# A chunk chain started behind its last input, row scalings moved from VectorE to ScalarE, and chunk states written and read back in parts

## The chip, the core and the metric

The kernel runs on one core of one Trainium2 chip. The engines named below are TensorE (PE in the profile), VectorE (DVE), ScalarE (ACT), GpSimd (POOL) and SyncE (SP), which here only issues DMAs. The metric is the device time of one execution in microseconds (us), as the median of several runs; lower is better.

## What is computed

One layer, all in float32: `x = x + attention(layernorm(x))`, then `x = x + ffn(layernorm(x))`, for 4 sequences of 1024 tokens and 128 features. The attention is a gated delta rule with 16 heads of 8 features, a recurrence over the tokens on an 8x8 state for each head:

```
def step(S, inp):
    qt, kt, vt, at, gft = inp
    bs1 = einsum('bhk,bhkv->bhv', kt, S)
    S1 = S + at[..., :, None] * bs1[..., None, :]
    S2 = exp(gft)[..., None] * S1
    bs2 = einsum('bhk,bhkv->bhv', kt, S2)
    S3 = S2 + at[..., :, None] * bs2[..., None, :] + kt[..., :, None] * vt[..., None, :]
    return (S3, einsum('bhk,bhkv->bhv', qt, S3))
_, o = lax.scan(step, S0, ...)
z = zeros_like(o)
out = stack([z, z, o], axis=2).reshape(B, 3 * N, H, HD)[:, -N:]
out = layernorm(out * gate) * ln_w @ Wout
...
# ffn: 16 experts, one for each token, and a shared one
scores = sigmoid(logits) * one_hot(top_1(logits))
masked_inputs = scores.T[:, :, None] * x[None, :, :]
gate, up = split(masked_inputs @ gate_up_proj[e])
expert_out = (up * silu(gate)) @ down_proj[e]
shared = silu(x @ w_gate.T) * (x @ w_up.T) @ w_down.T
```

Because of the stack and the slice, only the last 342 tokens' `o` are used, and they land in every third output row. In the other two thirds of the rows ("others") the attention adds nothing, so their FFN can run before the attention has ended. The rows that get an `o` are called "mixed".

## The kernel before, in words

**Chunks.** Each sequence is cut into 32 chunks (`C`), so that 4 x 32 chunks fill the 128 partitions. A chunk has 21 tokens of the first part (`L1`) and 11 of the second (`L2`), 32 steps (`NT`) in all. What a chunk does to the state that enters it is an 8x8 matrix and an added sum for each head, and these don't depend on the entering state. So 32 steps build all chunks' matrices and sums at once, in region 0 (21 steps) and in region 1 (11 steps). The last step ends with VectorE writing the last matrices (`next_state`, L1451, tile `state`), GpSimd multiplying the last sums (L978) and TensorE adding them up (`add_sum`, L1839); ScalarE then copies the sums out (`copy_sums`, L845), and SP stores and reloads matrices and sums through DRAM (L612 to L629).

**The chunk chain.** 63 serial steps m = 1 to 63 then carry the true state from chunk to chunk. For each, VectorE multiplies (L1527, from `ch_m` and `ch_s` to `ch_pr`) and reduces (L1532, to the next column of `ch_s`); GpSimd copies the chunk's sum into `ch_pr` (L1088). The copy for step m may go once step m-2 is reduced, since `ch_pr` has two buffers. Steps 1 to 32 use region 0's matrices (loaded some 80 us earlier), steps 33 to 63 region 1's. At the end the 32 states at which the second part begins, columns 0 to 31 of `ch_s`, go to DRAM and back in another layout into `state` (L1094, L1099, both issued by GpSimd), and the 11 steps with outputs begin (`products`, L1405; on TensorE `forward`, L1931 to L1934).

**What runs beside it.** The 22 tiles of "others" rows (128 rows of 128) are handled in six groups, five of 4 tiles and one of 2, by the shared expert: TensorE transposes the rows (L1798), ScalarE copies them (L830), TensorE multiplies by gate and up weights in two halves (L1810, L1811), ScalarE takes the silu (L835), VectorE multiplies (`shared_h`, L1296), TensorE multiplies by the down weights (L1820) and VectorE adds to the result (`shared_add`, L1301). VectorE's part is put between chain steps by `beside(m - 3)`: in every five steps of the chain, from m = 3 on, two `shared_h` and, two steps later, one `shared_add`. From m = 36 on, every third step has a `gate` (L1310 twice) of the expert pairs `RUNS[0]`, 12 pairs, of which the last two come after step 63.

**The rows that go to the experts.** Each of the 22 tiles is scaled by its score (L1500, VectorE, ahead of the chain) into room in `decayed` (8 tiles, part of the tile `grown`), `vterm` (8, part of `uv`) and `state` (6), and scattered by an indirect DMA that GpSimd issues (`scatter_tile`, L993), one behind each of GpSimd's first 22 chain copies. SP loads the expert pairs (L509) when all 22 scatters have landed; TensorE starts them (L1868) when the last `shared_add` is done.

**What sets the order.** Every engine runs its own program in the order in which it is written, and waits for semaphores. There is no scheduler. Ahead of the chain, ScalarE waits for `s_bout`, the landing of the stored sums (L625), and TensorE for `s_bc`, the copy of the sums. VectorE waits for `s_ba`, the last `add_sum`, because `vterm` is read by it.

## Time and profile before

| | us |
|---|---|
| median of 3 runs | 670.8 |
| lowest, highest | 670.62, 671.29 |
| the profiled execution's own time | 673.13 |
| its span, first to last instruction | 671.4 |
| chunk chain with what stands ahead of it, last state written to first product | 320.48 to 431.24 |

The span is what the profile's rows add up to. A row of the timeline gives the start, the duration (with merged instructions as one piece), the engine, the line, and in brackets how long the engine had been idle and which instruction ended that. The chain of waits is followed back from the last instruction, each step to what released it.

### The profile page before, as it was taken

The numbers are of one execution on the slowest core, as the hardware profiler recorded it, in microseconds if no ns is written. First come the engines' busy times: TensorE is split into PE (matmuls) and PEld (weight loads), VectorE is DVE, ScalarE is ACT, GpSimd is POOL, SyncE is SP. The second block draws the span as 40 slices with busy tenths as digits, with TensorE's granted clock in tenths as the row PEclk, the third lists the DMA queues.
The fourth block names the chain that finished last, engine by engine and source line by source line (L and its number), as shares of the span: only waits on it lengthen the run. The fifth ranks groups of instructions, "written<-read, shape, count | busy, mean of one in ns | idle before, by whom it ended". The sixth has DMA issues, their size and how long they took to land.

```text
span 671.4 us, 7382 instructions
## 1 busy us (share of the span) xinstructions
PE 528.3 (79%) x1809; PEld 273.7 (41%) x1810; DVE 492.5 (73%) x809; ACT 248.9 (37%) x515; POOL 360.0 (54%) x349
## 2 busy tenths in 40 slices
PE   1768989999999886877387689879999967578930
PEld 1434434444454433322154455525454255345520
DVE  3369999989898998799589999498999775412201
ACT  1825754444445242111122145533545124135520
POOL 4235767666667575654567333366767574700023
PEclk9868999999999998887799799998999977979985
DMA  9601116700000590000611012300100021112224
GB/s 218 138 0 32 32 42 162 217 0 1 0 1 0 141 356 35 1 0 0 170 35 55 17 48 69 110 15 16 31 23 18 0 52 35 43 56 63 63 80 111
DMA packets 46706, 41.79 MB, mean 62 GB/s; under 512 B 4588, under 2 KB 40248, under 8 KB 46168
## 3 DMA queue, kind: packets, MB, share of 16 engines
q1 hardware_dynamic: 43140, 35.61, 18.9%
q0 software_dynamic: 2400, 5.38, 2.7%
q10 hardware_dynamic: 1136, 0.46, 0.3%
q8 instruction: 12, 0.20, 0.1%
q14 instruction: 18, 0.15, 0.1%
HBM read 23.80 MB, written 17.63 MB: 62 GB/s over the span
## 4 chain that ended last, share of the span: by engine, by line
DVE 33%; PE 30%; issue 16%; POOL 12%; DMA 5%; ACT 2%; ACTq 1%; POOLq 0%; DVEq 0%; SPq 0%
DVE grown L1412 9%; PE ps L1874 6%; DVE early L1527 5%; POOL grown L1062 4%; DVE ps L1451 4%; PE ps L1831 4%; PE ps L1891 3%; DVE early L1532 3%; PE ps L1832 2%; PE ps L1931 2%; DVE grown L1439 2%; POOL uv L978 2%; PE ps L1639 2%; DVE grown L1405 2%; POOL early L1009 2%
## 5 line engine op out<-in xcount | busy, mean ns | idle before, releaser
L1062 POOL TENSOR_TENSOR grown<-grown 128x512 f32<-128x512 f32 x64 | 80.8, 1272 | 101.4 <-DVE grown L1439 101.4
L1412 DVE TENSOR_TENSOR grown<-ps,steps 128x1536 f32<-128x1536 f32 x64 | 112.1, 1752 | 1.8
L1831 PE MATMUL ps<-grown,cst 128*128 128x512 f32 x128 | 77.7, 692 | 27.8 <-DVE grown L1412 27.6
L857 ACT ACTIVATE uv<-ps 128x512 f32<-128x512 f32 x64 | 38.1, 597 | 110.5 <-DVE grown L1439 110.5
L1874 PE MATMUL ps<-steps 128*128 x128 | 69.6, 642 | 8.8 <-issue 8.6
L1832 PE MATMUL ps<-grown,cst 128*128 128x512 f32 x128 | 71.4, 641 | 0.0
L978 POOL TENSOR_TENSOR uv<-uv,steps 128x512 f32<-128x512 f32 x64 | 67.7, 1081 | 1.7 <-ACT uv L857 1.6
L1310 DVE TENSOR_TENSOR e_h<-rk,ps 128x256 f32<-128x256 f32 x64 | 25.4, 417 | 53.8 <-ACT rk L870 34.0
L1839 PE MATMUL ps<-uv,cst 128*128 128x512 f32 x128 | 60.4, 594 | 0.4 <-POOL uv L978 0.4
L1117 POOL TENSOR_TENSOR early<-state,qT 128x512 f32 x22 | 37.2, 1690 | 32.4 <-DVE state L1426 32.4
L1088 POOL COPY early<-early 128x32 f32<-128x32 f32 x63 | 27.5, 436 | 43.9 <-DVE early L1532 43.9
L1439 DVE TENSOR_TENSOR grown<-ps,steps 128x512 f32<-128x512 f32 x64 | 43.3, 677 | 9.3 <-PE ps L1831 9.2
L1831 PEld LDWEIGHTS ps<-grown,cst 128*128 128x128 f32 x128 | 22.7, 208 | 62.4 <-DVE grown L1412 56.2
L1451 DVE TENSOR_TENSOR ps<-ps,grown 128x512 f32<-128x512 f32 x60 | 41.6, 694 | 8.4 <-POOL grown L1062 8.4
L1445 DVE TENSOR_TENSOR ps<-ps,steps 128x512 f32<-128x512 f32 x64 | 44.1, 690 | 2.7 <-PE ps L1832 2.7
L1009 POOL DMA_INDIRECT early<-ys_mixed,slots_mixed x11 | 10.5, 959 | 64.8 <-DMA ys_mixed<-e_y 61.8
L1832 PEld LDWEIGHTS ps<-grown,cst 128*128 128x128 f32 x128 | 26.8, 209 | 35.4 <-issue 35.4
L1527 DVE TENSOR_TENSOR early<-early 128x256 f32<-128x256 f32 x63 | 39.4, 626 | 1.3
L870 ACT ACTIVATE rk<-ps 128x256 f32<-128x256 f32 x64 | 23.9, 384 | 40.7 <-PE ps L1874 39.7
L1891 PE MATMUL ps<-steps,e_hT 128*128 x256 | 35.9, 283 | 2.7 <-ACT e_hT L874 2.7
L1839 PEld LDWEIGHTS ps<-uv,cst 128*128 128x128 f32 x128 | 24.2, 190 | 31.8 <-issue 29.8
L1891 PEld LDWEIGHTS ps<-steps,e_hT 128*128 128x128 f32 x256 | 31.5, 191 | 9.1 <-issue 8.0
(221 smaller groups left out, 1001.8 us busy)
## 6 DMA issues: line engine op xcount, KB each, us to landing
steps<-gate_up_proj SPq DMA_DIRECT2D x1, 4096.0 KB, 15.3
xs_others<-zeros SPq DMA_DIRECT2D x1, 2496.0 KB, 10.9
steps<-xs_others SPq DMA_DIRECT2D x19, 128.0 KB, 2.1
ys_others<-e_y SPq DMA_DIRECT2D x19, 128.0 KB, 1.9
early<-chain_m SPq DMA_DIRECT2D x4, 512.0 KB, 6.3
xf<-x SPq DMA_DIRECT2D x4, 495.0 KB
normed<-early SPq DMA_DIRECT2D x28, 64.0 KB, 1.7
xs_mixed<-zeros SPq DMA_DIRECT2D x1, 1728.0 KB, 8.9
```

Of the source, the lines that this page charges most:

```text
L978: return G.tensor_tensor(wide(dst, w), wide(src, w), per_col(tile, k, 1, h, w), ALU.mult)
L1062: G.tensor_tensor(decayed[:, h], decayed[:, h], work[:, h, 1], ALU.add).then_inc(s_add[h], 1)
L1412: V.tensor_tensor(grown[:, :, h].rearrange("p e (x w) -> p e x w", w=HD), st, per_col(tile, FF, 3, h, HD), ALU.mult).then_inc(s_prod[h], 1)
L1439: V.tensor_tensor(wide(work[:, h, 1], HD), wide(ps[h][:, 1], HD), per_col(tile_of(i), PP, 1, h, HD), ALU.mult).then_inc(s_uterm[h], 1)
L1445: V.tensor_tensor(wide(bank[2 * h], HD), wide(bank[2 * h], HD), per_col(tile_of(i), K, 1, h, HD), ALU.mult).then_inc(s_term[h], 1)
L1451: V.tensor_tensor(dst, bank[2 * h], decayed[:, h], ALU.add).then_inc(s_state[h], 1)
L1527: V.tensor_tensor(ch_pr[:, m % 2, :, :, 0:HD], ch_m[r][:, :, i, :].rearrange("p j i -> p i j").unsqueeze(1) .to_broadcast([P, 4, HD, HD]), ...
L1831: T.matmul(bank[2 * h + 1], c["block"], work[:, h, 1], start=True, stop=True).then_inc(s_usum[h], 1)
L1832: T.matmul(bank[2 * h], c["minus"], work[:, h, 0], start=True, stop=True).then_inc(s_red[h], 1)
L1839: T.matmul(bank[4 + h], c["ident"], vterm[:, h], start=i in (0, L1), stop=i + 1 in (L1, NT)).then_inc(s_ba[h], 1)
L1874: T.matmul(b_gu(run, b)[u], e_xT[:, b, u], gu[:, bass.ds(ex * (2 * F), 2 * F)], start=True, stop=True).then_inc(s_eg, 1)
L1891: ins = T.matmul(b_y(run)[:, u * D:(u + 1) * D], e_hT[:, u, f * P:(f + 1) * P], dw[:, bass.ds(ex[u] * F + f * D, D)], start=(f == 0), stop ...
```

## The change

1. The 22 scalings leave VectorE. ScalarE does them (`scaled_rows`): four behind the first group's copy of the transposed rows, and four (at last two) behind the two silus of each group.
2. VectorE's wait for `s_ba`, `s_score` and `s_rows` ahead of the chain is gone; it waits for the last states and the loaded x, and begins the chain.
3. ScalarE no longer waits for `s_bout`. It waits instead for both last states, the scores and the rows. A silu on one column (`warm`) stands ahead of `copy_sums`.
4. TensorE's wait for `s_bc` moves behind the shared expert; its first gate matmul waits for the last states and the last copies of region 1.
5. GpSimd's scatters stand behind the copies of steps 2 to 5, 6 to 9, 11 to 14, 16 to 19, 21 to 24, 26 and 27 (`SCATTER_AT`), rather than behind 1 to 22.
6. The chunk states go out in three parts: columns 0 to 15 behind copy 50, 16 to 27 behind copy 62, 28 to 31 at the end. They come back in two: 0 to 15 behind copy 54, 16 to 31 at the end. VectorE waits for both (32 rather than 16).

```diff
@@ scalar engine
+            def scaled_rows(lo):
+                q = fb[OTHERS.name]
+                for j in range(lo, min(lo + 4, OTHERS.n)):
+                    if j == 4 * HALF // D:
+                        act.wait_ge(s_mout, 32)
+                    S.activation(q["scaled"][j], q["shared"][j], ACT.Copy, scale=q["score"][:, j:j + 1]).then_inc(s_sc, 1)
+
             def shared(t):
...
                         S.activation(xT_shared(t, g), b_xT(t, g)[:, 0:w], ACT.Copy).then_inc(s_fx, 1)
+                        if g == 0:
+                            scaled_rows(0)
                     for k in (0, 1):
...
                         S.activation(f_silu[t.name][:, 0:w], b_gate[k][:, 0:w], ACT.Silu).then_inc(s_fsg, 1)
+                    if t is OTHERS:
+                        scaled_rows(4 * g + 4)
...
                 front(i)
+            S.activation(warm[:, 2:3], eps[:], ACT.Silu)
             copy_sums(ucopy)
-            act.wait_ge(s_bout, 32)
+            for h in (0, 1):
+                act.wait_ge(s_state[h], NT + 2)
+            act.wait_ge(s_score, 1)
+            act.wait_ge(s_rows, 16 * 6 * B)
@@ gpsimd
+            SCATTER_AT = [j + 2 if j < 4 else SHARED_EVERY * (j // 4) + j % 4 + 1 for j in range(OTHERS.n)]
+            ENDS = (0, C // 2, C - 4, C)
+
+            def starts_out(k):
+                cols = slice(4 * ENDS[k], 4 * ENDS[k + 1])
+                G.dma_start(scr["s"].rearrange("(l i) x -> l i x", i=HD)[:, :, cols],
+                            ch_s[:, :, ENDS[k]:ENDS[k + 1], :].rearrange("l i c v -> l i (c v)")).then_inc(s_sout, 16)
+
+            def starts_in(lo, hi):
+                cols = slice(4 * ENDS[lo], 4 * ENDS[hi])
+                pool.wait_ge(s_sout, 16 * hi)
+                pool.wait_ge(s_mout, 32)
+                pool.wait_ge(s_scat[OTHERS.name], 16 * OTHERS.n)
+                G.dma_start(state[:].rearrange("p v (b x) -> p (v b) x", b=B)[:, :, cols],
+                            scr["s"].rearrange("(g q) x -> q g x", q=P)[:, :, cols]).then_inc(s_chout, 16)
...
-                if m <= OTHERS.n:
-                    scatter_tile(OTHERS, m - 1)
+                if m in SCATTER_AT:
+                    scatter_tile(OTHERS, SCATTER_AT.index(m))
+                if m == C + ENDS[1] + 2:
+                    starts_out(0)
+                if m == C + ENDS[1] + 6:
+                    starts_in(0, 1)
+                if m == C + ENDS[2] + 2:
+                    starts_out(1)
             pool.wait_ge(s_ca, 2 * C + 1)
-            pool.wait_ge(s_mout, 32)
-            G.dma_start(scr["s"].rearrange("(l i) x -> l i x", i=HD),
-                        ch_s[:, :, 0:C, :].rearrange("l i c v -> l i (c v)")).then_inc(s_sout, 16)
-            pool.wait_ge(s_sout, 16)
-            pool.wait_ge(s_scat[OTHERS.name], 16 * OTHERS.n)
-            G.dma_start(state[:].rearrange("p v (b x) -> p (v b) x", b=B),
-                        scr["s"].rearrange("(g q) x -> q g x", q=P)).then_inc(s_chout, 16)
+            starts_out(2)
+            starts_in(1, 3)
@@ vector engine
-            dve.wait_ge(s_score, 1)
-            dve.wait_ge(s_rows, 16 * 6 * B)
             dve.wait_ge(s_xf, 16 * 3 * B)
             for h in (0, 1):
-                dve.wait_ge(s_ba[h], NT + 1)
                 dve.wait_ge(s_state[h], NT + 2)
-            q = fb[OTHERS.name]
-            for j in range(OTHERS.n):
-                if j == 4 * HALF // D:
-                    dve.wait_ge(s_mout, 32)
-                V.tensor_scalar(q["scaled"][j], q["shared"][j], q["score"][:, j:j + 1], None, ALU.mult
-                                ).then_inc(s_sc, 1)
...
-            dve.wait_ge(s_chout, 16)
+            dve.wait_ge(s_chout, 32)
@@ tensor engine, shared(t)
                 if t is OTHERS:
                     transposes(0)
+                    for h in (0, 1):
+                        pe.wait_ge(s_state[h], NT + 2)
+                        pe.wait_ge(s_uc[h], NT + 1)
...
+            shared(OTHERS)
             pe.wait_ge(s_bc, 2)
-            shared(OTHERS)
```

On ScalarE, from the last copy of the last step to the second group. Before:

```order
L857 ACTIVATE uv<-ps 128x512 [waits s_bp0,s_uterm0]
L845 ACTIVATE uv<-ps 128x1024 [waits s_ba1,s_bp1,s_bp0,s_ba0]
L830 ACTIVATE grown<-ps 128x512 [waits s_b_out,s_f_transposed]
L835 ACT_TABLE_LOAD
L835 ACTIVATE grown<-ps 128x512 [waits s_f_gate_up]
L835 ACTIVATE grown<-ps 128x512 [waits s_f_h,s_f_gate_up]
L830 ACTIVATE grown<-ps 128x512 [waits s_f_transposed]
```

And in the changed kernel, where L858 is the copy of the sums, L839 that of the transposed rows, L831 the scaling and L846 the silu:

```order
L870 ACTIVATE uv<-ps 128x512 [waits s_bp0,s_uterm0]
L872 ACT_TABLE_LOAD
L872 ACTIVATE warm<-eps 128x1
L858 ACTIVATE uv<-ps 128x1024 [waits s_ba1,s_bp1,s_bp0,s_ba0]
L839 ACTIVATE grown<-ps 128x512 [waits s_rows_in,s_score,s_state0,s_state1,s_f_transposed]
L831 ACTIVATE grown<-early,score_others 128x128 x4
L846 ACTIVATE grown<-ps 128x512 [waits s_f_gate_up]
L846 ACTIVATE grown<-ps 128x512 [waits s_f_h,s_f_gate_up]
L831 ACTIVATE grown<-early,score_others 128x128 x4
L839 ACTIVATE grown<-ps 128x512 [waits s_f_transposed]
```

The table load moved ahead of the sums' copy, the wait for the stored sums (`s_b_out`) is gone, and eight scalings stand in the first group's stretch.

On VectorE, from the last state to the first `shared_h`. Before:

```order
L1451 TENSOR_TENSOR state<-ps,grown 128x512 [waits s_add0,s_term0,s_m_out]
L1500 TENSOR_SCALAR grown<-early,score_others 128x128 [waits s_state0,s_ba0,s_ba1,s_xf,s_state1,s_rows_in,s_score]
L1500 TENSOR_SCALAR grown<-early,score_others 128x128 x7
L1500 TENSOR_SCALAR uv<-early,score_others 128x128 x8
L1500 TENSOR_SCALAR state<-early,score_others 128x128 [waits s_m_out]
L1500 TENSOR_SCALAR state<-early,score_others 128x128 x5
L1515 MEMSET early 128x8x4
L1527 TENSOR_TENSOR early<-early 128x32x8 [waits s_sums_in,s_matrices_in,s_chain_state,s_uc1,s_uc0]
L1532 TENSOR_REDUCE early<-early 128x4x8 [waits s_chain_sums,s_chain_mul]
```

In the changed kernel (L1486 is the state, L1551 and L1556 the chain's multiplication and reduction, L1331 `shared_h`):

```order
L1486 TENSOR_TENSOR state<-ps,grown 128x512 [waits s_add0,s_term0,s_m_out]
L1539 MEMSET early 128x8x4 [waits s_state1,s_state0,s_xf]
L1551 TENSOR_TENSOR early<-early 128x32x8 [waits s_sums_in,s_matrices_in,s_chain_state,s_uc1,s_uc0]
L1556 TENSOR_REDUCE early<-early 128x4x8 [waits s_chain_sums,s_chain_mul]
L1551 TENSOR_TENSOR early<-early 128x32x8 [waits s_chain_state]
L1556 TENSOR_REDUCE early<-early 128x4x8 [waits s_chain_sums,s_chain_mul]
L1551 TENSOR_TENSOR early<-early 128x32x8 [waits s_chain_state]
L1556 TENSOR_REDUCE early<-early 128x4x8 [waits s_chain_sums,s_chain_mul]
L1331 TENSOR_TENSOR grown<-grown,ps 128x512 [waits s_f_silu]
```

The 22 scalings are gone; the chain's steps and the first `shared_h` behind step 3 stand as before.

On GpSimd, at the end of the chain. Before:

```order
L993 DMA xs_others<-state,slots_others 4992x128 [waits s_scaled]
L1088 COPY early<-early 128x32 [waits s_chain_state,s_sums_in] x41
L1094 DMA chain_s<-early 1024x1x128 [waits s_m_out,s_chain_state]
L1099 DMA state<-chain_s 128x8x128 [waits s_scattered_others,s_s_out]
L1106 UNCONDITIONAL_BRANCH [waits s_scattered_others]
```

In the changed kernel (L1010 the scatter, L1123 the copy, L1103 a part out, L1112 a part in):

```order
L1010 DMA xs_others<-state,slots_others 4992x128 [waits s_scaled]
L1123 COPY early<-early 128x32 [waits s_chain_state,s_sums_in] x23
L1103 DMA chain_s<-early 1024x1x64
L1123 COPY early<-early 128x32 [waits s_chain_state,s_sums_in] x4
L1112 DMA state<-chain_s 128x8x64 [waits s_scattered_others,s_m_out,s_s_out]
L1123 COPY early<-early 128x32 [waits s_chain_state,s_sums_in] x8
L1103 DMA chain_s<-early 1024x1x48
L1123 COPY early<-early 128x32 [waits s_chain_state,s_sums_in]
L1103 DMA chain_s<-early 1024x1x16 [waits s_chain_state]
L1112 DMA state<-chain_s 128x8x64 [waits s_scattered_others,s_m_out,s_s_out]
```

Three of the five transfers stand among the chain's copies; the one that is left to go out at the end has rows of 16 elements (64 bytes) rather than 128, and the one that comes back rows of 64.

## Rows read from the trace of the kernel before

**Rows 1.** The page's first row.

```profile
span 671.4 us, 7382 instructions
```

**Rows 2.** Chain of waits from the last state on: start, duration, what.

```profile
319.79 0.70 DVE state L1451
...
324.63 8.07 DMA chain_b<-uv
332.81 0.61 ACT grown L830
```

**Rows 3.** Timeline of that stretch: start, duration, instruction, [idle before <-releaser].

```profile
320.82 2.16 PE L1839 MATMUL ps<-uv,cst 128*128 128x512 f32 x4 [0.42 <-POOL uv L978]
321.74 0.24 POOL L1088 COPY early<-early 128x32 f32<-128x32 f32 x1
323.01 1.02 ACT L845 ACTIVATE uv<-ps 128x1024 f32<-128x1024 f32 x1 [4.08 <-PE ps L1839]
323.27 1.78 DVE L1500 TENSOR_SCALAR grown<-early,score_others 128x128 f32<-128x128 f32 x8 [2.79 <-PE ps L1839]
323.85 1.19 POOL L993 DMA_INDIRECT xs_others<-grown,slots_others  x1 [1.87 <-DVE grown L1500]
...
337.90 0.69 DVE L1296 TENSOR_TENSOR grown<-grown,ps 128x512 f32<-128x512 f32 x1 [6.61 <-ACT grown L835]
...
340.27 0.69 DVE L1296 TENSOR_TENSOR grown<-grown,ps 128x512 f32<-128x512 f32 x1 [0.64 <-ACT grown L835]
```

**Rows 4.** Stretches: length, busy of PE, PEld, DVE, ACT, POOL; PEclk, DMA share, GB/s.

```profile
325.00:327.00 2.00, 0.00 (x0) 0.00 (x0) 2.00 (x12) 0.00 (x0) 1.29 (x3) 1.00 0.99 229
333.00:335.00 2.00, 1.54 (x2) 0.84 (x3) 0.00 (x0) 1.69 (x2) 0.64 (x1) 0.50 0.51 133
422.70:425.20 2.50, 2.50 (x17) 1.82 (x15) 0.84 (x2) 1.64 (x4) 0.00 (x0) 1.00 0.85 256
```

**Rows 5.** Timeline of the shared expert's second group and the start of its third.

```profile
342.90 1.02 PE L1810 MATMUL ps<-grown,wT 128*128 128x512 f32 x2
344.82 0.60 ACT L835 ACTIVATE grown<-ps 128x512 f32<-128x512 f32 x1 [4.09 <-PE ps L1811]
346.67 0.60 ACT L835 ACTIVATE grown<-ps 128x512 f32<-128x512 f32 x1 [1.25 <-DVE grown L1296]
350.12 1.02 PE L1810 MATMUL ps<-grown,wT 128*128 128x512 f32 x2
```

**Rows 6.** ScalarE's scalings of the mixed rows, late in the kernel: timeline.

```profile
559.23 3.32 ACT L964 ACTIVATE early<-early,score_mixed 128x128 f32<-128x128 f32 x11
```

**Rows 7.** Groups by line, 338.5 to 421.4: busy us, mean ns | idle before, releaser.

```profile
L1527 DVE TENSOR_TENSOR early<-early 128x256 f32<-128x256 f32 x60 | 37.5, 626 | 1.1
L1532 DVE TENSOR_REDUCE early<-early 128x32 f32<-128x288 f32 x60 | 27.3, 454 | 2.1
```

**Rows 8.** Timeline: first pair's load and transposes, and the chain's end.

```profile
367.03 0.90 SPq L509 DMA_DIRECT2D steps<-xs_others  x2
379.98 0.66 PE L1868 MATMUL ps<-cst,steps 128*128 128x128 f32 x2 [1.39 <-DVE xf L1301]
...
420.94 0.45 DVE L1532 TENSOR_REDUCE early<-early 128x32 f32<-128x288 f32 x1
421.69 0.92 POOL L1094 DMA_DIRECT2D chain_s<-early  x1 [1.80 <-DVE early L1532]
431.24 3.27 DVE L1405 TENSOR_TENSOR grown<-state,steps 128x1024 f32<-128x1024 f32 x2 [2.18 <-DVEq L1540]
432.61 1.10 PE L1931 MATMUL ps<-grown,cst 128*128 128x512 f32 x2 [0.76 <-DVE grown L1405]
```

**Rows 9.** DMA issues: out<-in, queue, count, KB each, us from issue to landing.

```profile
chain_s<-early POOLq DMA_DIRECT2D x1, 512.0 KB, 4.1
state<-chain_s POOLq DMA_DIRECT2D x1, 512.0 KB, 4.9
...
xs_others<-state,slots_others POOLq DMA_INDIRECT x6, 2.3
```

More of the change, by code:

```diff
@@ L205, in build @@
         eps = sb("eps", [P, 1])
+        warm = sb("warm", [P, 3])
         early = sb("early", [P, L2 * COLS])
```

## The prediction

> **What bounds the kernel now.** I read the chain of waits first, since it names the stretch that the change touches. It runs from the last state (written at 319.79, done at 320.48) not into the chunk chain but into a store: the sums land 8.07 us after their issue at 324.63, and only then does ScalarE copy the first transposed rows, at 332.81 [rows 2]. The timeline shows what that does to VectorE [rows 3]. It idles 2.79 us from its last state until TensorE's last `add_sum` has ended (320.82 + 2.16 = 322.98), scales 22 tiles, and makes three chain steps. Then it stands 6.61 us in front of the first `shared_h`, which starts at 337.90, and 0.64 us in front of the second at 340.27. Behind that VectorE is full: in 60 steps its chain instructions take 37.5 + 27.3 us with 1.1 and 2.1 us of idle time before them [rows 7]. So from 340.27 to the last reduction's end at 421.39 [rows 8] VectorE sets the pace, and all that is won ahead of the first `shared_h` should arrive at the end of the chain. The stretch behind it is two DMAs in series: issue at 421.69, 4.1 us, issue again, 4.9 us, first product at 431.24 [rows 8, 9]. The last expert pairs run beside them on TensorE: it is free at 432.61 - 0.76 = 431.85 [rows 8].
>
> **Part 1, the start of the chain (edits 1 to 4): 10.65 us.** The first `shared_h` needs the later of two paths.
>
> The silu's path. ScalarE copies the sums from 323.01 to 324.03 as now, since that waits for TensorE until 322.98 and not for anything that changed. The 1.3 us table load and the one-column silu sit in the 4.08 us that ScalarE is idle before it [rows 3]. The transposes of the first rows have nothing but 322.98 ahead of them and four small matmuls to do, so they are done before 324.03. The copy of the rows takes 0.61 [rows 2]: 324.64. From TensorE's first gate matmul to the silu's start are 1.92 us in the second group (344.82 - 342.90), and the silu takes 0.60 [rows 5]. So: 324.64 + 0.03 + 1.92 + 0.60 + 0.05 = 327.25. The four scalings lie in ScalarE's wait for those matmuls: 11 took 3.32 us, 0.30 each, so four end at 324.64 + 1.25 = 325.9, before the silu could start at 326.6 [rows 6].
>
> GpSimd's path. Its copy for step 3 now stands behind the first scatter, and this waits for the first scaling, ready at 325.0. The first scatter took 1.19 and a copy 0.24 [rows 3], and a reduction 0.45 [rows 7]. So: 325.0 + 1.2 + 0.25 + 0.1 + 0.45 = 327.0. Steps 1 and 2 are done by then: step 1 can't be reduced before its copy, which GpSimd does at 321.74 as now [rows 3], and two steps of 1.16 us follow.
>
> The later path gives 327.25 against 337.90: **10.65 us** earlier. It matters that TensorE is at full clock. In the trace the granted clock is still 1.00 (2.4 GHz) at 325 to 327, with TensorE idle, and 0.50 (1.2 GHz) at 333 to 335, where the first gate matmuls ran [rows 4]. The changed kernel has them at 324.7 to 328.1, so I take the full clock; the other case is a rival.
>
> **Part 2, the second `shared_h`: 0.6 us.** Its wait of 0.64 came from those slow matmuls. At full clock the second silu starts at 324.67 + 2 x 1.72 + 0.2 = 328.3 and ends at 328.9. VectorE comes there 2.37 - 0.64 = 1.73 us after the first one's start, at 328.98 [rows 3]. So the wait goes: 0.6.
>
> **Part 3, the steady groups: 0.** What is added to ScalarE in each group is 1.25 us between the second silu and the copy for the next group. That silu ends at 347.27, so the copy would end at 347.27 + 1.25 + 0.61 = 349.1; TensorE is busy with the down weights until 350.12 anyway [rows 5]. That cover is 1.0 us; without it each of five groups would be late by the rest. GpSimd's scatters fall from five in five steps to four. The last one moves from copy 22 to copy 27, five steps and three products or some 8 us later; SP, whose next work is the pairs' load, has it at 367.03 now and would have it at about 375, while TensorE needs it at 379.98 [rows 8]: 2 us of cover with the load itself. The 22 scalings leave VectorE, but that is in part 1 and is not counted twice.
>
> **Part 4, the parts that go out and back among the chain's steps: 0.** Three more issues of 0.92 each on GpSimd [rows 8]. Behind copies 50, 54 and 62 the next copy may slip by up to 0.5 us, but VectorE wants it only two steps, 2.3 us, later; if the copies were wanted at once, this would cost 1.5 us. The first part comes back four steps after it went, some 6 us against the 4.1 that the whole one took [rows 9].
>
> **Part 5, the tail: 0.7 us.** The last part out has as many rows as before (1024), of 64 bytes rather than 512, and the one back 1024 rows of 256. Nothing in the trace moves such rows. Out: not under 2.3 us, a scatter of 128 rows [rows 9], and at least 4.1 if the cost is one of rows; the bus was 0.85 busy for 2.5 us there [rows 4], so bytes are a part of it. I take 3.5 out and 4.4 back, nearer to the whole transfers than to the scatter, as the row count is theirs. That is 1.1 us less, to the first product at 430.1 in the clock of before. But TensorE is free only at 431.85, and starts at 432.61 now: at most **0.76** can be won however short the DMAs are, because the last pair keeps its distance to the chain. I take 0.7. If rows of 64 bytes cost more than whole ones, this is a loss; doubling the 2.5 us of out gives 6.6 + 4.9, 2.5 us later than now.
>
> On this the Trainium skill speaks against the change: "DMA: Bandwidth & Descriptors", section Specifications, gives 512 B as the smallest transfer at line rate and says that below it the DMA engine does a read-modify-write. No row here shows it; by it part 5 is at best nothing and may be the loss just priced.
>
> **Sum.** 10.65 + 0.6 + 0.7 = 11.95, say 12.0 us. The span of 671.4 [rows 1] becomes 659.4. The profiled execution took 673.13, 2.3 above the median of 670.8, so the shift is applied to the median: **658.8 us**.
>
> **Rivals.**
> A. *Slow clock at the first group.* For: the clock falls to 0.50 in this stretch. Against: with TensorE idle it did so only after 327. Then `shared_h` comes 4.48 us behind the copy of the rows, as it did (337.90 - 333.42) [rows 2, 3], at 324.64 + 4.48 = 329.12, and the second wait stays: 8.8 + 0.7 = 9.5 us, 661.3.
> B. *Small rows in the tail.* No gain to a loss of 2.5 us: 11.25 - (0 to 2.5), 659.5 to 662.0.
> C. *Given back in the middle.* ScalarE's or GpSimd's order makes groups late: a scaling is nearer 0.385 than 0.30, copies slip behind scatters whose scalings come late. With 0.3 us in each of five groups and 0.5 at the first steps, 2 us: 660.8.
> D. *Slower than before.* ScalarE becomes the bound of the shared expert: four scalings stand between silu and copy, and VectorE's in-order chain waits at each `shared_h`. To eat 12.0 + 1.3 us in five groups takes 2.7 us each on top of the 1.0 of cover, so 1.25 + 3.7 = 4.9 us for four scalings, 1.2 each; the row says 0.30. At 1.3 each the time is 673.
> E. *It doesn't do what it says*, since the chain at step 33 would stand for region 1's matrices. The stored sums land at 332.7 [rows 2] and are loaded back directly behind; step 33 comes half-way through the chain, some 35 us later: excluded as far as these rows go.
>
> **How the numbers follow.** Forecast (657.5 to 659.8) 0.58; A 0.12; B beyond 659.8 0.12; C 0.12; D 0.02; more gain than forecast 0.02; no change by an unseen new wait 0.02. The range leaves out the outer parts of A to D: 657.3 to 662.0. A measurement of this kernel can tell about 0.2%, 1.3 us, from no change. Faster by more 0.96, within 0.02, slower 0.02.
>
> **What would show it.** Right: VectorE's first chain multiplication within 0.5 us of the last state; the first `shared_h` near 327.3 with a wait of 0.2 to 3 us in the last chain step or before it; TensorE's clock 1.00 from 324 on; no wait before later `shared_h`; the last reduction near 410.1; from there to the first product 9.1 us or less, with TensorE's first `forward` matmul directly behind the last pair. Wrong: a first `shared_h` near 329 at clock 0.50 (A); more than 10 us between last reduction and product (B); ScalarE named as releaser of several `shared_h`, or VectorE idle in front of reductions with GpSimd as releaser (C, D).

## The result

The changed kernel takes 660.23 us (659.72 to 664.59, 4 runs) against 670.71 (669.66 to 671.29, 4 runs) for the kernel before: ratio 0.9858, 95% interval 0.9821 to 0.9896. (The ratios here are the recorded estimates; the quotient of the two medians is 0.9844, inside that interval.) 658.8 was predicted, with a range of 657.3 to 662.0: the time lies inside the range, but 0.4 us beyond the prediction's own narrow band of 657.5 to 659.8. Its profiled execution took 659.8 us. One run of all that follow, 677.68 us in e10, was in a slower state and is left out of its median. The span below answers to [rows 1].

Page of the changed kernel, first row:

```profile
span 657.7 us, 7388 instructions
```

The two spans differ by 13.7 us, more than the medians (10.5). A trace starts at the first instruction, so I measure from the last state's write on: 319.79 before [rows 2], 317.95 after. These 1.84 us lie ahead of the stretch that the change is meant to shorten, and nothing shows that they are its own: the same mark is at 317.22 and 318.90 in two more traces of the changed kernel (e6, e11) and at 317.61 in e5, whose edit begins behind it. From the last state to the first new state of the second part it is 117.67 us before and 106.16 after: **11.51 us** in the changed stretch. Behind that point the two traces differ by 0.35.

Timeline of the changed kernel from the last state to the second `shared_h` (start, duration, instruction, idle time before it and what ended that). It answers to [rows 3]:

```profile
317.12 1.28 ACT L872 ACT_TABLE_LOAD   x1
...
317.95 0.69 DVE L1486 TENSOR_TENSOR state<-ps,grown 128x512 f32<-128x512 f32 x1
...
318.99 1.39 DVE L1551 TENSOR_TENSOR early<-early 128x256 f32<-128x256 f32 x1
...
321.10 1.02 ACT L858 ACTIVATE uv<-ps 128x1024 f32<-128x1024 f32 x1 [2.48 <-PE ps L1866]
...
322.50 1.27 ACT L831 ACTIVATE grown<-early,score_others 128x128 f32<-128x128 f32 x4
...
322.75 1.10 PE L1837 MATMUL ps<-grown,wT 128*128 128x512 f32 x2 [1.26 <-ACT grown L839]
...
323.19 1.19 POOL L1010 DMA_INDIRECT xs_others<-grown,slots_others  x1 [2.56 <-ACT grown L831]
...
324.39 0.25 POOL L1123 COPY early<-early 128x32 f32<-128x32 f32 x1
...
324.74 0.45 DVE L1556 TENSOR_REDUCE early<-early 128x32 f32<-128x288 f32 x1 [1.88 <-POOL early L1123]
324.75 0.60 ACT L846 ACTIVATE grown<-ps 128x512 f32<-128x512 f32 x1 [0.98 <-PE ps L1838]
...
325.38 0.69 DVE L1331 TENSOR_TENSOR grown<-grown,ps 128x512 f32<-128x512 f32 x1 [0.18 <-ACT grown L846]
...
327.09 0.69 DVE L1331 TENSOR_TENSOR grown<-grown,ps 128x512 f32<-128x512 f32 x1
```

The chain begins 1.04 us behind the last state rather than 8.09. The two `shared_h` start 7.43 and 9.14 us behind it, where they started 18.11 and 20.48 behind it [rows 2, 3]. The 6.61 us wait has become one of 1.88 for GpSimd in step 3 and one of 0.18 for ScalarE.

The same kernel in stretches of 2 us (columns: length, busy time of PE, PEld, DVE, ACT, POOL, then the granted TensorE clock, DMA share, GB/s). It answers to [rows 4], whose 333 to 335 had the clock at 0.50:

```profile
324.00:326.00 2.00, 2.00 (x6) 0.90 (x5) 1.08 (x3) 0.60 (x1) 1.86 (x4) 1.00 0.96 225
326.00:328.00 2.00, 1.03 (x6) 0.53 (x5) 1.97 (x5) 1.54 (x5) 1.74 (x4) 1.00 0.93 204
```

VectorE's groups by line from the second `shared_h` to the chain's end, as in [rows 7]:

```profile
L1551 DVE TENSOR_TENSOR early<-early 128x256 f32<-128x256 f32 x59 | 36.9, 626 | 1.1
L1556 DVE TENSOR_REDUCE early<-early 128x32 f32<-128x288 f32 x60 | 27.3, 454 | 3.0 <-POOL early L1123 1.1
```

Idle time in front of reductions grew from 2.1 to 3.0 us, and now names GpSimd's copies. The way from the second `shared_h` to the last reduction's end is 81.79 us long, where it was 81.12.

The tail, as in [rows 8]; the second fence is what the profile says of the parts' DMAs, to set beside [rows 9]:

```profile
409.17 0.84 POOL L1103 DMA_DIRECT2D chain_s<-early  x1 [1.82 <-DVE early L1556]
...
412.33 0.90 POOL L1112 DMA_DIRECT2D state<-chain_s  x1 [2.32 <-DMA chain_s<-early]
...
416.64 3.26 DVE L1440 TENSOR_TENSOR grown<-state,steps 128x1024 f32<-128x1024 f32 x2 [0.66 <-DVEq L1564]
...
418.81 0.38 ACT L896 ACTIVATE e_y<-ps 128x256 f32<-128x256 f32 x1 [1.45 <-PE ps L1918]
...
419.24 1.12 PE L1958 MATMUL ps<-grown,cst 128*128 128x512 f32 x2 [0.47 <-ACT e_y L896]
```

```profile
L1103 POOL DMA_DIRECT2D chain_s<-early x3: 845/852/914, 389.5 to 409.2; - x3
...
DMA to landing us min/median/max: 2.9/3.3/3.4
```

The first product comes 7.76 us behind the last reduction's end (9.85 before), but TensorE's first `forward` matmul comes 10.36 behind it (11.22 before). It is released by ScalarE's last copy of the last expert pair (`e_y`), not by the product.

The stretch adds up: 10.68 (first `shared_h`) + 0.66 (second) - 0.67 (middle) + 0.86 (to `forward`) = 11.53 of the 11.51 us.

### The profile page after: what moved, and what is told of

It is laid out like the page before. It is cut to its first block, busy times and chain, and to the rows that moved or that the text cites. A ratio compares the mean times of both kernels' runs of the same rounds, so it can differ in the third digit from the quotient of the medians.

```text
span 657.7 us, 7388 instructions
## 1 busy us (share of the span) xinstructions
PE 518.7 (79%) x1809; PEld 268.9 (41%) x1810; DVE 488.9 (74%) x787; ACT 255.3 (39%) x538; POOL 363.0 (55%) x352
## 4 chain that ended last, share of the span: by engine, by line
PE 35%; DVE 28%; issue 14%; POOL 12%; DMA 5%; ACT 2%; ACTq 1%; POOLq 0%; DVEq 0%; SPq 0%
DVE grown L1447 9%; PE ps L1901 9%; PE ps L1918 5%; DVE ps L1486 4%; POOL grown L1079 4%; PE ps L1858 4%; PE ps L1908 2%; DVE early L1551 2%; PE ps L1859 2%; DVE grown L1474 2%; PE ps L1958 2%; POOL uv L995 2%; POOL early L1026 2%; PE ps L1663 2%; PE ps L1959 2%
## 5 line engine op out<-in xcount | busy, mean ns | idle before, releaser
L1858 PE MATMUL ps<-grown,cst 128*128 128x512 f32 x128 | 76.3, 680 | 29.4 <-DVE grown L1447 29.3
L1859 PE MATMUL ps<-grown,cst 128*128 128x512 f32 x128 | 69.7, 628 | 0.0
L1486 DVE TENSOR_TENSOR ps<-ps,grown 128x512 f32<-128x512 f32 x60 | 41.6, 693 | 8.3 <-POOL grown L1079 8.3
L1123 POOL COPY early<-early 128x32 f32<-128x32 f32 x63 | 27.3, 435 | 27.9 <-DVE early L1556 27.8
L1551 DVE TENSOR_TENSOR early<-early 128x256 f32<-128x256 f32 x63 | 40.2, 638 | 1.3
```

The source lines that it names most:

```text
L1486: V.tensor_tensor(dst, bank[2 * h], decayed[:, h], ALU.add).then_inc(s_state[h], 1)
L1551: V.tensor_tensor(ch_pr[:, m % 2, :, :, 0:HD], ch_m[r][:, :, i, :].rearrange("p j i -> p i j").unsqueeze(1) .to_broadcast([P, 4, HD, HD]), ...
L1858: T.matmul(bank[2 * h + 1], c["block"], work[:, h, 1], start=True, stop=True).then_inc(s_usum[h], 1)
L1859: T.matmul(bank[2 * h], c["minus"], work[:, h, 0], start=True, stop=True).then_inc(s_red[h], 1)
```

## The experiments

All are compared by the same marks, in us behind the last state: first `shared_h`, last reduction's end, first `forward` matmul, first new state. Times come with the kernel before on the same chip; "the changed kernel" without more is the first trace of it, above. Each kernel has one trace, and stretches that an edit doesn't touch differ between traces by up to 0.4 us, which will matter below. e1 to e4 ran on one chip, e5 to e8 on a second, e9 to e12 on a third.

| kernel | `shared_h` | chain's end | `forward` | new state |
|---|---|---|---|---|
| before | 18.11 | 101.60 | 112.82 | 117.67 |
| changed | 7.43 | 90.93 | 101.29 | 106.16 |
| e1_wait_only | 11.22 | 96.08 | 106.86 | 111.70 |
| e2_parts_only | 17.84 | 101.49 | 112.27 | 117.15 |
| e3_wait_back | 17.69 | 101.63 | 112.43 | 117.30 |
| e4_no_parts | 7.43 | 91.08 | 101.68 | 106.53 |
| e5_filler | 16.29 | 99.03 | 109.81 | 114.66 |
| e6_changed_again | 7.55 | 92.44 | 102.85 | 107.72 |
| e11_changed_third | 7.51 | 92.39 | 102.72 | 107.59 |
| e8_one_step | 7.43 | 89.21 | 99.63 | 104.50 |
| e7_two_steps | 7.52 | 89.47 | 99.78 | 104.65 |
| e12_two_steps_again | 7.73 | 89.65 | 100.01 | 104.88 |
| e9_scatters_later | 7.49 | 89.87 | 100.21 | 105.08 |
| e10_pairs_sooner | 7.43 | 90.47 | 101.69 | 106.56 |

**e3_wait_back: the changed kernel with one wait put back.**

```diff
             copy_sums(ucopy)
+            act.wait_ge(s_bout, 32)
             for h in (0, 1):
                 act.wait_ge(s_state[h], NT + 2)
```

> The changed kernel with ScalarE's wait for the stored sums put back ahead of its copy of the transposed rows; scalings stay on ScalarE, all else as changed. Theory: VectorE makes the chain's first two steps at once, but the first shared_h comes again about 17 to 18 us behind the last state, with TensorE at clock 0.50, so all of the 11.3 us at the start is lost, though VectorE has no scaling to do: 670 to 671. Rival (taking 4.7 us of scalings from VectorE has a worth of its own): about 666.

Measured: 671.46 us (12 runs), ratio 1.0001 (0.998 to 1.0021). One wait takes back the whole change. (Edits 1, 2, 4, 5 and 6 are all still in this kernel.) Timeline of this kernel on ScalarE and VectorE:

```profile
330.65 0.60 ACT L839 ACTIVATE grown<-ps 128x512 f32<-128x512 f32 x1 [8.52 <-DMA chain_b<-uv]
331.15 1.27 ACT L831 ACTIVATE grown<-early,score_others 128x128 f32<-128x128 f32 x4
```

```profile
333.38 0.46 DVE L1557 TENSOR_REDUCE early<-early 128x32 f32<-128x288 f32 x1 [10.53 <-POOL early L1124]
335.81 0.69 DVE L1332 TENSOR_TENSOR grown<-grown,ps 128x512 f32<-128x512 f32 x1 [1.98 <-ACT grown L846]
```

ScalarE stands for the stored sums, the scalings behind it too, GpSimd's scatter behind those and step 3's copy behind the scatter: VectorE, freed of 22 scalings, waits 10.53 us instead. Without that wait gone, moving the scalings and all the rest are worth nothing.

**e1_wait_only: the kernel before with that wait replaced, and nothing else.** The scalings stay on VectorE.

```diff
             copy_sums(ucopy)
-            act.wait_ge(s_bout, 32)
+            for h in (0, 1):
+                act.wait_ge(s_state[h], NT + 2)
...
                     transposes(0)
+                    for h in (0, 1):
+                        pe.wait_ge(s_state[h], NT + 2)
+                        pe.wait_ge(s_uc[h], NT + 1)
```

> The kernel before, with ScalarE's wait for the stored sums replaced by the wait for the last states (and TensorE's first gate matmul waiting for the last states and copies); the 22 scalings stay on VectorE, ahead of the chain, and nothing else changes. Theory (the wait for the stored sums is what VectorE stands for, and the scalings are a second, separate price behind it): the first silu is ready at about 327, VectorE comes to the first shared_h only at 331.3, behind scalings and three steps, and doesn't wait; the second wait of 0.64 goes too: 6.6 + 0.6 = 7.2 us faster, 663.5. Rival (it is the scalings ahead of the chain that cost, and the wait is only cover for them): within 1 us of the kernel before.

Measured: 666.92 us (7 runs), ratio 0.9935 (0.9906 to 0.9964), 4.5 us faster. In the stretch it is 5.97, of which 5.52 are there at the chain's end; the other 0.45 lie in the tail, which this edit leaves alone. Expected were 7.2. The first `shared_h` came as expected (11.22, no wait), but TensorE, ready early, then stood idle for 3.97 us until VectorE's second `shared_h`, and its clock fell. Timeline and stretches of this kernel, columns as above:

```profile
333.86 3.78 PE L1824 MATMUL ps<-wT,grown 128*128 128x128 f32 x16 [3.97 <-DVE grown L1297]
```

```profile
337.68 0.69 DVE L1302 TENSOR_TENSOR xf<-xf,ps 128x512 f32<-128x512 f32 x1 [1.70 <-PE ps L1824]
```

```profile
331.00:333.00 2.00, 0.00 (x0) 0.00 (x0) 1.93 (x5) 0.72 (x2) 1.74 (x5) 0.84 0.73 254
335.00:337.00 2.00, 2.00 (x11) 2.00 (x10) 0.94 (x2) 0.00 (x0) 1.86 (x4) 0.50 0.92 287
```

With TensorE idle at 331 to 333 the clock fell on its way to 0.50, which is the lower of its two levels (1.2 GHz). The down matmuls took 3.78 us in place of the changed kernel's 2.05, so `shared_add` waited 1.70. The other 5.15 us of the chain's end (96.08 against 90.93) are what moving the scalings is worth once the wait is gone, the clock included: the second part of the change pays only when the first is made.

**e5_filler: what the slow clock costs.** The kernel before, with nine matmuls of a block of zeros (128x512; 18 instructions in the trace, 7.89 us in all) written over a bank that nothing reads then, so that TensorE isn't idle while the sums are stored.

```diff
                     transposes(0)
+                    for _ in range(9):
+                        T.matmul(b_tok, c["ident"], zeros[:], start=True, stop=True)
```

> The kernel before with nine matmuls of zeros (512 columns each, into a free PSUM bank) behind TensorE's transposes of the first rows, so that it works from 325 to about 332.5 while ScalarE waits for the stored sums. The wait itself, the scalings and all else stay. Theory (the first gate matmuls were slow because TensorE had stood idle and its granted clock was 0.50): clock 1.00 at 333 to 335, the first shared_h 2.6 us behind ScalarE's copy of the rows rather than 4.5, no wait before the second, 2.5 us less between the last state and the chain's end (99.1 rather than 101.6), and about 2.5 us in the time, 669. Rival (these matmuls take their time for another reason, their operands or the DMAs beside them): they keep 0.86 us a piece and nothing moves.

Measured: 680.88 us (12 runs) against 683.37 (17 runs) on this chip, ratio 0.9961 (0.9932 to 0.9989). Stretches and timeline of this kernel:

```profile
333.00:335.00 2.00, 2.00 (x7) 0.92 (x6) 1.09 (x2) 0.60 (x2) 0.00 (x0) 1.00 0.49 139
```

```profile
333.90 0.69 DVE L1296 TENSOR_TENSOR grown<-grown,ps 128x512 f32<-128x512 f32 x1 [4.69 <-ACT grown L835]
...
335.62 0.69 DVE L1296 TENSOR_TENSOR grown<-grown,ps 128x512 f32<-128x512 f32 x1
```

With TensorE kept busy the clock was 1.00 where it had been 0.50 [rows 4]; the first `shared_h` came 1.82 us sooner, the wait before the second was gone, and the chain ended 2.57 sooner. So, as an estimate from this run, 1.8 + 0.65 us of the prediction's 11.25 in parts 1 and 2 are the clock's. In the changed kernel they come with the earlier start: TensorE idles only 1.26 us ahead of its gate matmuls there, and the clock was 1.00.

**e2_parts_only and e4_no_parts: the states' way out and back.** e2 is the kernel before with `starts_out` and `starts_in` as in the change; e4 is the changed kernel with the whole transfers of before at the end.

```diff
-            starts_out(2)
-            starts_in(1, 3)
+            pool.wait_ge(s_mout, 32)
+            G.dma_start(scr["s"].rearrange("(l i) x -> l i x", i=HD),
+                        ch_s[:, :, 0:C, :].rearrange("l i c v -> l i (c v)")).then_inc(s_sout, 16)
...
```

> The kernel before, with only the chunk states sent out in three parts and back in two (edit 6). Theory (the last expert pair, not the two DMAs, sets when TensorE begins the last stage): VectorE's first product comes 2.1 us earlier behind the last reduction, but ScalarE's last copy of the last pair ends 10.9 us behind that reduction as before, so the kernel gains 0 to 0.4 us, 670.5. Rival (the DMAs in series set it): 2.1 us, 668.6. If the small rows were dearer than whole ones: slower.

> The changed kernel with the chunk states sent out and back whole at the chain's end, as before. Theory (TensorE's and ScalarE's last pair nearly covers the DMAs): 0.3 to 0.9 us slower than the changed kernel. Rival (the parts bring their whole 2.1 us): 2 us slower.

Measured: e2 672.59 us (12 runs), ratio 1.0008 (0.9985 to 1.0031). e4 661.18 us (6 runs), ratio 0.9843 (0.9818 to 0.9868), not to be told apart from the changed kernel's ratio. In the traces the way from the chain's end to the new state is 16.07 us before and 15.66 in e2, 15.45 in e4 and 15.23 in the changed kernel. But e1 and e5 send the states whole, as before, and have 15.62 and 15.63: the 0.4 us between before and e2 are a trait of that one trace of before, and e2's parts gained nothing. Against e4 the parts gain 0.22, under what the medians can show. The tail of e4:

```profile
407.79 0.91 POOL L1112 DMA_DIRECT2D chain_s<-early  x1 [1.82 <-DVE early L1539]
411.92 0.94 POOL L1117 DMA_DIRECT2D state<-chain_s  x1 [3.22 <-DMA chain_s<-early]
...
416.72 3.26 DVE L1423 TENSOR_TENSOR grown<-state,steps 128x1024 f32<-128x1024 f32 x2 [1.94 <-DVEq L1547]
...
418.09 1.10 PE L1941 MATMUL ps<-grown,cst 128*128 128x512 f32 x2 [0.52 <-ACT e_y L896]
```

Even with whole transfers and the product 1.47 us later, `forward` is released by the last pair's copy (`e_y`): the last pair is the bound, and shorter transfers only lengthen VectorE's lead on it. In before, e1 and e5 the product was the later of the two, but by 0.2 to 0.35 us only.

**e6_changed_again and e11_changed_third: the changed kernel twice more.**

> The changed kernel again, to see which times its executions take beside those of the kernel before on one chip: 660 to 661, and stretches from the last state to the chain's end (90.9) and to the first new state (106.2) as in its first trace, since they depend on nothing ahead of them.

> The changed kernel once more, so that its time and trace stand beside the others of this call on the same chip. Ratio to the kernel before 0.980 to 0.987 as in its two earlier runs (0.986 and 0.980); last reduction 90.9 us behind the last state if TensorE's clock is at its full level in the first two groups, 92.4 if it falls there as in the second run.

Measured: 669.85 us (6 runs), ratio 0.9798 (0.977 to 0.9827), and 670.80 us (5 runs) against 682.55, ratio 0.9824 (0.9789 to 0.9858). In both the chain ended 1.5 us later behind the last state than in the first trace, which for e6 was not expected. The first fence is the first trace, the second is e6:

```profile
332.00:334.00 2.00, 1.76 (x8) 0.76 (x6) 1.76 (x4) 0.24 (x1) 1.87 (x4) 1.00 0.96 262
334.00:336.00 2.00, 0.27 (x2) 0.28 (x3) 1.79 (x4) 2.00 (x6) 1.87 (x3) 1.00 0.18 53
336.00:338.00 2.00, 2.00 (x17) 1.81 (x17) 1.72 (x5) 0.24 (x1) 1.74 (x5) 1.00 0.10 33
```

```profile
332.00:334.00 2.00, 1.16 (x6) 0.50 (x4) 1.59 (x4) 0.57 (x2) 1.81 (x3) 1.00 1.00 264
334.00:336.00 2.00, 0.85 (x7) 0.85 (x8) 1.74 (x4) 1.67 (x6) 1.81 (x3) 0.99 0.16 51
336.00:338.00 2.00, 2.00 (x11) 2.00 (x11) 1.34 (x3) 0.00 (x0) 1.85 (x3) 0.50 0.10 33
```

From 332 to 336 TensorE was busy for 2.03 us in one and for 2.01 in the other; in one the clock stayed, in the other it fell to half for the second group's down matmuls, and VectorE stood 0.85 us in front of the `shared_add` behind them (the profile names no releaser for that wait). It is rival A's mechanism one group later, and it differs between runs of one program; why it falls in one and not in the other stays open. Of the nine traces with the early start and the scalings on ScalarE, four have it (e6, e11, e7, e12).

**e9_scatters_later: the loss in the middle.** The changed kernel with each scatter one chain step later.

```diff
-            SCATTER_AT = [j + 2 if j < 4 else SHARED_EVERY * (j // 4) + j % 4 + 1 for j in range(OTHERS.n)]
+            SCATTER_AT = [j + 3 if j < 4 else SHARED_EVERY * (j // 4) + j % 4 + 2 for j in range(OTHERS.n)]
```

> The changed kernel with GpSimd's scatters of the first expert's rows one chain step later each and nothing else. Asked: what of the 1.5 us by which the run with one more step ahead (e8_one_step) ended its chain earlier is GpSimd's order. Theory S (scatters): the reduction of step 3 then waits for ScalarE's scaling through GpSimd's copy no longer, so its wait of 1.88 us shrinks to under 0.8 and the first shared_h stays where it is (7.4 us behind the last state, since ScalarE's silu bounds it), while the seven waits of reductions for GpSimd's copies (3.2 us in all) halve: last reduction 0.5 to 1.0 us earlier relative to the last state than the changed kernel run beside it. Theory N: the waits sit in slack and nothing moves, under 0.3 us.

Measured: 669.74 us (5 runs) against 670.80 for the changed kernel beside it, ratio to before 0.9799 (0.9763 to 0.9836). The waits of VectorE from the last state to the chain's end (engine, line, what it waited for: us in total, times, longest), the changed kernel first, then e9:

```profile
DVE early L1556 <- POOL early L1123: 3.2, 7, 1.9
DVE e_h L1345 <- ACT rk L887: 0.3, 1, 0.3
DVE grown L1331 <- ACT grown L846: 0.2, 1, 0.2
```

```profile
DVE grown L1331 <- ACT grown L846: 2.0, 1, 2.0
DVE state L1486 <- POOL grown L1079: 0.3, 1, 0.3
DVE early L1556 <- POOL early L1123: 0.2, 1, 0.2
```

Seven waits for GpSimd's copies become one. The 1.88 only changes its name, since the silu bounds the first `shared_h` anyway, and the 0.21 at the first step is there in both. The other five, 0.21 to 0.24 each, were real; they lie in the first two groups, and one of them reads so in the changed kernel:

```profile
330.67 0.62 DVE L1551 TENSOR_TENSOR early<-early 128x256 f32<-128x256 f32 x1
330.72 0.68 POOL L1123 COPY early<-early 128x32 f32<-128x32 f32 x1
331.50 0.45 DVE L1556 TENSOR_REDUCE early<-early 128x32 f32<-128x288 f32 x1 [0.21 <-POOL early L1123]
```

A scatter has pushed the copy into the time of VectorE's multiplication. There it takes 0.68 us instead of 0.25 and ends 0.11 behind the multiplication (331.29), and the reduction waits for it. Against the first trace, the one with the same clock, the chain ends 1.06 us sooner (89.87 against 90.93), which is what the five waits come to. That the medians also differ by 1.06 is chance: the trace of the changed kernel beside e9 (e11) had the half clock in the second group, and the intervals would also allow no difference.

**e8_one_step, e7_two_steps, e10_pairs_sooner, e12_two_steps_again: using the slack ahead of the first `shared_h`.** e8 makes one more chain step ahead of it, e7 and e12 two; their scatters and pairs' slots move with it, and TensorE's wait for the attention's first result stands behind the first pair's gate and up matmuls. e10 is the changed kernel with that wait moved, alone. The edit of e7 and e12:

```diff
-        BEGIN, SHARED_EVERY, PAIRS_FROM, PAIR_EVERY = 3, 5, 33, 3
+        BEGIN, SHARED_EVERY, PAIRS_FROM, PAIR_EVERY = 5, 5, 31, 3
...
-            SCATTER_AT = [j + 2 if j < 4 else SHARED_EVERY * (j // 4) + j % 4 + 1 for j in range(OTHERS.n)]
+            SCATTER_AT = [j + 4 if j < 4 else SHARED_EVERY * (j // 4) + j % 4 + 3 for j in range(OTHERS.n)]
...
                 for u in range(U):
                     gate_up(run, 0, 0, 0, u)
+                if run is RUNS[0]:
+                    pe.wait_ge(s_fa, NOG)
                 over_pairs(pe, run, pair)
...
-            pe.wait_ge(s_fa, NOG)
             pe.wait_ge(s_we, 48)
```

> As the kernel with two steps, but one: shared_h from step 4 on, scatters one copy later, first gate four steps behind the last shared_add. Theory: 1.2 us earlier at the first shared_h for the same chain step, first gate waits under 1 us: chain's end at about +89.8, 659.5. Rival: as there.

> The changed kernel with the shared expert's part of VectorE two chain steps later (first shared_h behind step 5 rather than 3), the scatters two copies later, the gates of the pairs at the same chain steps as now (36, 39, ...), and TensorE's wait for the last shared_add moved from ahead of the first pair's transposes to ahead of its first transposes into the shared bank. Theory (VectorE stands 1.9 us in step 3 for a copy that GpSimd makes only behind the first scatter, which waits for ScalarE's first scaling): steps 3 to 5 are made in that time, the first shared_h comes at +7.7 us behind the last state but two steps further, and the chain's end comes 1.3 to 2.0 us earlier than in the changed kernel (at +89 to 89.6), less what the first gate waits for TensorE, 0 to 1.6: 658.5 to 660. Rival (the room between the last shared_add and the first gate, three steps rather than five, costs more than it brings): the first gate waits over 2 us and the chain ends no earlier.

> The changed kernel with one wait of TensorE moved: the one for the attention's first result (s_fa) now stands behind the gate and up products of the first expert pair instead of ahead of them; nothing else. Theory W: VectorE's waits in front of its first e_h (two for TensorE, 3.1 us in all, and three for ScalarE, 1.9) shrink and the last reduction comes 0.5 to 1.0 us earlier relative to the last state; theory N: those products wait for the same sums as before and nothing moves, under 0.3 us. If neither this run nor e9_scatters_later moves the end, the gain of e7_two_steps and e8_one_step comes from the step made ahead of the first shared_h itself.

> The kernel of e7_two_steps again (two steps more ahead of the first shared_h, scatters two steps later, pairs' groups two steps earlier, the wait for the attention's first result behind the first gate and up products), to see if it is faster than the changed kernel beside it. If its chain's end 1.5 us earlier is real, it is 1.0 to 2.0 us faster by the medians; if it was the clock of one run, within 0.5 us.

Measured: e8 668.72 us (6 runs), ratio 0.9772 (0.9735 to 0.9808); e7 667.80 (6 runs), 0.9763 (0.9729 to 0.9798); both beside the changed kernel's 669.85. e12 668.99 (5 runs), 0.9809 (0.9781 to 0.9836), beside 670.80. So by the medians two steps beat the changed kernel by 2.05 and 1.81 us on two chips, with overlapping intervals each time. The first `shared_h` hardly moves: the steps fit into the 1.88 us that VectorE stood there. One step gives 1.72 us at the chain's end with the second group's clock full in both traces. Not all of it is the step's: 1.26 us are there after step 33, where e10 has gained nothing, and the rest comes behind it, where e10 gains its 0.46 too. e8's scatters stand where e9's do in the chain, but `shared_h` has moved along with them, and so seven waits for GpSimd's copies are back (2.0 us in all): e9's gain isn't in it. Two steps give 2.7 to 3.0 against traces with the same half clock in the second group. e10 took 670.41 us (4 runs, beside 670.80), with a recorded ratio of 0.9861 (0.9814 to 0.9908): its chain ends 0.46 us sooner, but the last pair ends 0.39 later, and `forward` comes 0.40 later. Moved alone, that wait wins nothing in the time. A kernel with both e12's steps and e9's later scatters wasn't run.

## Why the prediction was right, and where it wasn't

**What bounds the kernel.** Right: e3 shows that with the wait for the stored sums left in, nothing is won. But the wait isn't the whole of it, since the scalings stood in a row with it: e1 shows that taking the wait away with the scalings left brings 5.97 of 11.5 us, e3 that moving them without it brings none. The table load that moved ahead (edit 3) was not run alone. ScalarE stood only 0.98 us in front of the first silu, so a load of 1.28 there would have cost some 0.3 us; that is an estimate from the rows above.

**Part 1, 10.65 us.** Measured 10.68. By its steps, behind the last state: silu's end 7.41 worked out and 7.40 measured; step 3's reduction done 7.21 worked out and 7.24 measured; four scalings 1.25 and 1.27. One thing was not in it. VectorE's first multiplication ran 1.39 us rather than 0.63, while GpSimd multiplied the last sums in SBUF (317.77 to 319.88). At the first step it cost nothing, since step 3 waited later. The Trainium skill, "SBUF — State Buffer", section "Who interferes with whom", says that a VectorE instruction with two inputs in SBUF and a GpSimd instruction that reads SBUF contend for one pair of ports, and that one of them is blocked until the other is done; the traces agree. The multiplication took 0.76 us more than its usual 0.63, and in e6 and e9, where it took 1.50 and 1.45, it ended 0.5 us behind GpSimd's, as in the first trace. The other way round, GpSimd's copies grow from 0.25 to 0.68 us beside VectorE's multiplications; that did cost something, in part 3.

**Clock (rival A).** Right for the first group in every trace of the changed kernel, and e5 prices the mechanism at 2.57 us at the chain's end. But I checked only one group. The second group's clock fell in two of the changed kernel's three traces (four of nine with its variants), for 1.5 us at the chain's end. That the first trace was the one without it is luck; with the fall the stretch's gain would have been 10 us instead of 11.5 (107.72 in e6 against 117.67). It belongs to part 3.

**Part 2, 0.6 us.** Measured 0.66.

**Part 3, 0.** This is the term that failed; it was put at nothing: 0.67 lost in the first trace, 2.05 in e6 with the fall of the clock (92.44 - 9.27 against 81.12). ScalarE's cover held; no later `shared_h` waits. GpSimd's did not: I followed its scatters for when the last one lands and not for the copies behind them. In a group of five steps four scatters of 1.0 to 1.35 us stand between copies that VectorE wants every 1.16 us. GpSimd stands 2.56 us for the first scaling before it can begin them, and then works almost without a pause until the third group, so that its copies fall beside VectorE's multiplications; e9 gets 1.06 back by shifting them. It is rival C's "copies slip behind scatters", at half its size or less. The sign that the prediction had named for it, reductions waiting for GpSimd, is there.

**Part 4, 0.** No wait of the chain names a part's issue. Right as far as the traces go; e4, without them, ends its chain 90.93 + 0.15 behind the last state.

**Part 5, 0.7 us.** Measured 0.86, so the number fits, but for another reason and in part by luck. The DMAs were shorter than taken (2.9 out where I took 3.5; 4.1 back where I took 4.4): the product comes 7.76 us behind the chain's end rather than 8.7. But the cap was misread. I took TensorE as free 0.76 us before `forward`; it also needs ScalarE's copy of the last pair, which ended only 0.34 before it. Of the 0.86 us, 0.57 come from pairs that ended that much sooner relative to the chain. And 0.44 of the 0.86 need none of the change: `forward` comes 10.78 us behind the chain's end in e1 and e5, which have the whole transfers of before, against 11.22 in the one trace of before. What the parts bring is 0 (e2) to 0.2 us (e4). Rival B is out: the last part's 1024 rows of 64 bytes landed in 2.9 us, and the whole transfer's rows of 512 took 4.1 [rows 9]. The read-modify-write that the Trainium skill, "DMA: Bandwidth & Descriptors", section Specifications, expects under 512 B is not to be seen in a time: here eight times fewer bytes took 1.2 us less. No run compares short and long rows at the same number of bytes.

**From sum to time.** 12.0 predicted, 11.5 in the stretch, 10.5 by the first medians. The rest lies outside the stretch. On the chips of e6 and e11 the same two kernels differed by 13.5 and 11.75 us, although the changed kernel's stretch was some 1.5 us longer there. What lies behind the new state varies from trace to trace on those chips: 247.5 us in e5, which is the kernel before but for its filler, 243.0 in e6, 241.2 in e8, 246.9 in e9. So the total is good to a few us at best, and the parts rest on the stretches. The prediction's "0.2%, 1.3 us" for what a measurement can tell was too fine: the 95% intervals here reach 0.2 to 0.5% to either side. The stretch behind the new state took 233.6 to 234.0 us in the traces of before, changed, e2 and e3, and 236.1 to 236.2 in those of e1 and e4, which is neither kernel's property.

## What to carry over

When one engine's in-order program waits for a transfer, list what else stands between its input and the next wait of the bottleneck: taking away one of them may give nothing (e3), another half (e1), both all. An engine's work that is moved beside another's can also make both slower: here GpSimd's copies went from 0.25 to as much as 0.68 us, and VectorE's first multiplication from 0.63 to 1.39. Work moved from the busiest engine to an idle one has to be followed to the third engine that consumes it, and every instruction queued behind that one has to be timed against its reader, in each group and not only at the last. Before a transfer is shortened, find the latest of all releasers of what follows; here it was a copy by an engine that the wait's first name did not show.

## What the hardware showed that I hadn't expected

**The same program, a different clock.** The granted clock along the span in 40 slices (tenths), changed kernel and e6, the same instructions:

```profile
PEclk9968999999999998899999799999999977889985
```

```profile
PEclk9889999999999998987989899989999956979975
```

**The same kernel, 12 us longer on two other chips.** The kernel before took 671.41 us on one chip (24 runs) and 683.37 and 682.55 on two others (17 and 9 runs); whether it is the chip or something else in those runs wasn't tested. From the last state to the new state the changed kernel is nearly the same everywhere but for the clock of one group (106.16, 107.72, 107.59 us). It is what follows that is longer: 233.6 us against 243.0 and 242.7. In the stretches there the changed kernel and e6 read:

```profile
545.00:585.00 40.00, 25.46 (x99) 15.29 (x100) 17.46 (x37) 12.54 (x29) 17.51 (x16) 0.81 0.14 41
585.00:625.00 40.00, 35.82 (x180) 22.93 (x179) 8.42 (x20) 19.82 (x50) 0.00 (x0) 1.00 0.21 63
```

```profile
545.00:585.00 40.00, 23.12 (x97) 16.27 (x97) 14.68 (x34) 10.28 (x22) 15.86 (x17) 0.76 0.12 33
585.00:625.00 40.00, 35.31 (x156) 21.34 (x156) 8.95 (x19) 17.61 (x44) 0.00 (x0) 0.91 0.19 57
```

The clock is lower there and less work is done by the same time. How much of the 9 us is the clock's, and how much is another thing's that makes TensorE idle first, was not taken apart.
